# Six expert-weight slots, shared norm statistics, tanh for sigmoid, the first conv tap on ScalarE, and new turn tables in an eight-layer kernel

## The reference, cut to what matters

```python
x = x + L0_attn(layernorm(x))   # proj 128 -> 2176; causal conv of 4 taps on 1024 channels, silu; SSD scan with
                                # state 64; times silu(z); norm over 1024; proj 1024 -> 128
x = x + L0_ffn(layernorm(x))    # xr, xk: mixes of x[t] and x[t-1]; sigmoid(xr Wr) * ((relu(xk Wk))^2 Wv)
h = layernorm(x)                # h is the input and the inner residual of the next layer
x = x + L1_attn(h)              # = h + mamba(norm(h)): conv of 4 taps on 256 channels, silu, 16 states per channel
x = x + L1_ffn(layernorm(x))    # 8 experts, top 2 of 8: gelu(x w1 + b1) w2 + b2
x = x + L2_attn(layernorm(x))   # linear attention with a running sum over tokens, 16 heads of 8
x = x + L2_ffn(layernorm(x))    # silu(x w1 s1) * (x w2 s2), gelu(h1), gelu(h2), w3
x = x + L3_attn(layernorm(x))   # silu(a) * sigmoid(b) -> xin; A, B, C from xin; scan with 16 states; rms norm; proj
x = x + L3_ffn(layernorm(x))    # 8 experts, top 2: (silu(x wg + bg) * (x wu + bu)) wd + bd
```

## Time and profile before

| | |
|---|---|
| three runs | 1398.04, 1400.70, 1400.92 us (median 1400.7) |
| span of the profiled execution | 1400.6 us; no time beyond its span is recorded for it |
| busy of the span | TensorE 1104.8, VectorE 890.9, ScalarE 630.4, GpSimd 281.7 us |
| moved | 107 MB |

### The profile page before, as it was taken

One profiled execution on the slowest core, in us unless ns is written; L12 is line 12 of the kernel. 1 busy time (PEld: TensorE's weight loads), 2 busy tenths in 40 slices (PEclk: granted clock), 3 DMA queues, 4 the chain that ended last, 5 costly groups with the idle time before them and its releaser, 6 DMA issues.

```text
span 1400.6 us, 15057 instructions
## 1 busy us (share of the span) xinstructions
PE 1104.8 (79%) x4959; PEld 698.7 (50%) x4959; DVE 890.9 (64%) x1919; ACT 630.4 (45%) x1194; POOL 281.7 (20%) x258
## 2 busy tenths in 40 slices
PE   4978657767977979686768676799999899897791
PEld 2536312334743634353457442574555556787781
DVE  6787879987558767767635789723735652363432
ACT  3433385424552348634237972273252434542330
POOL 3000113324120002130230244202000032014404
PEclk9999877777989999878889897999999999899996
DMA  8100000003520000000125420370000014468782
GB/s 322 47 0 1 0 0 0 0 1 118 163 61 1 0 0 1 0 0 0 45 92 177 131 74 21 96 224 21 1 1 0 1 63 132 157 214 283 260 277 69
DMA packets 49411, 107.02 MB, mean 76 GB/s; under 512 B 4840, under 2 KB 32368, under 8 KB 48688
## 3 DMA queue, kind: packets, MB, share of 16 engines
q1 hardware_dynamic: 44656, 92.74, 20.7%
q0 software_dynamic: 4096, 8.40, 2.0%
q10 hardware_dynamic: 576, 4.87, 0.8%
HBM read 91.24 MB, written 14.75 MB: 76 GB/s over the span
## 4 chain that ended last, share of the span: by engine, by line
PE 41%; DVE 22%; ACT 13%; issue 9%; POOL 7%; DMA 6%; SPq 1%; DVEq 0%; POOLq 0%; ACTq 0%
PE ps L1920 6%; PE ps L1638 5%; DMA expert_ring<-in_e_dram 4%; PE ps L1586 4%; PE ps L1752 4%; DVE up L1341 3%; PE ps L1858 3%; POOL slots_dram L717 3%; ACT big L957 2%; PE ps L1692 2%; PE ps L1829 2%; PE ps L1958 2%; DVE big L1348 2%; POOL up L727 2%; PE ps L1909 1%
## 5 line engine op out<-in xcount | busy, mean ns | idle before, releaser
L1858 PE MATMUL ps<-big,expert_ring 128*128 128x128 f32 x1160 | 158.0, 286 | 33.6 <-DMA expert_ring<-in_e_dram 20.4
L1858 PEld LDWEIGHTS ps<-big,expert_ring 128*128 128x128 f32 x1160 | 145.2, 199 | 48.0 <-DMA expert_ring<-in_e_dram 26.9
L1341 DVE TENSOR_TENSOR_SCAN up<-cv,big 128x512 f32<-128x512 f32 x128 | 152.5, 1230 | 21.5 <-ACT cv L908 17.4
L660 POOL TENSOR_TENSOR rstd<-ve,nhalf 128x4 f32<-128x4 f32 (+1 forms) x41 | 47.2, 1153 | 577.2 <-DVE ve L1119 470.6
L1752 PE MATMUL ps<-big,consts 128*128 128x512 f32 x256 | 154.3, 735 | 2.4 <-DVE big L1348 2.4
L697 POOL TENSOR_TENSOR big<-big,mt 128x512 f32<-128x512 f32 x64 | 85.8, 1344 | 279.1 <-ACT mt L901 152.6
L1920 PE MATMUL ps<-big,weights 128*128 128x512 f32 x256 | 115.4, 597 | 0.0
L1769 PE MATMUL ps<-q,row_pick 96*128 96x512 bf16 x128 | 54.5, 448 | 76.6 <-DVE big L1348 61.4
L1829 PE MATMUL ps<-expert_ring,big 128*128 128x128 f32 x792 | 107.6, 280 | 5.9 <-ACT big L957 3.6
L1829 PEld LDWEIGHTS ps<-expert_ring,big 128*128 128x128 f32 x792 | 98.9, 195 | 15.3 <-ACT big L957 9.8
L1459 DVE SCALAR_TENSOR_TENSOR big<-ps,expert_ring,key 128x128 f32<-128x128 f32 x184 | 51.8, 344 | 79.6 <-PE ps L1858 67.4
(11 more groups left out here) (247 smaller groups left out, 1943.4 us busy)
## 6 DMA issues: line engine op xcount, KB each, us to landing
expert_ring<-in_e_dram SPq DMA_DIRECT2D x46, 836.0 KB, 5.3
expert_ring<-in_e_dram SPq DMA_DIRECT2D x53, 578.0 KB, 4.4
big<-slots_dram SPq DMA_DIRECT2D x21, 256.0 KB, 3.5
results_dram<-mt SPq DMA_DIRECT2D x21, 256.0 KB, 5.3
weights<-in_w_dram ACTq DMA_DIRECT2D x1, 3072.0 KB, 15.5
slots_dram<-big SPq DMA_DIRECT2D x2, 1024.0 KB, 10.3
weights<-in_w_dram SPq DMA_DIRECT2D x1, 1600.0 KB, 8.6
x<-in_x_dram SPq DMA_DIRECT2D x4, 256.0 KB, 13.6
```

The lines of the kernel that those rows point to most:

```text
L1341: dve.tensor_tensor_scan(UP[s][:, j, PAD:PAD + T], CV[s][:, j, :], BIG2[s][:, j, :], 0.0, ALU.mult, ALU.add).then_inc(m_scan[s], 1)
L1858: last = pe.matmul(bank4(s, r if m else b % 2)[:, k, :], ring[:, q % RING, r * T + k * P:r * T + (k + 1) * P], XGT[s][:, b // 4 % 4, b % 4 ...
```

## The change

- Layer 7 may use six weight slots, four of the ring and two in the memory of the first weights (layers 0 and part of 1). `ring_plan` gives each load the slot whose last load is oldest; layer 3 keeps to four. A load waits for the result of the block that had the slot, or, for a spare slot's first use, for the end of layer 1 for the last samples.
- In layer 7 of stream 1 the odd blocks put gate and up into stream 0's banks, once stream 0 has made its last gated product. The waits for a free bank go back two blocks there.
- In layer 2 both norms come from one set of statistics of x: the second's variance is worked out as var (1 + eps) + eps^2. GpSimd does both powers from it.
- ScalarE does the first conv tap (scale and bias) for layers 0 and 2, right behind its copy to UP. VectorE does three taps.
- sigmoid(x) becomes tanh(x / 2) in layers 1 and 6; the 0.5 and + 1 go into instructions that follow, into W_A, W_B, W_C and the norm weight (scaled once), and into the mean of squares.
- Some yields that stood ahead of a wait alone are gone, and all turn tables are new.

```diff
+def ring_plan():
+    order, held, used, plan = expert_loads(), [None] * (RING + SPARE), [0] * (RING + SPARE), {}
+    place = {load: k for k, load in enumerate(order)}
+    for load in order:
+        slots = range(RING + SPARE * load[0])
+        slot = min(slots, key=lambda k: -1 if held[k] is None else place[held[k]])
+        used[slot] += 1
+        plan[load] = slot, used[slot], held[slot]
+        held[slot] = load
+    return plan
...
+        def expert_slot(m, s, b):
+            slot = plan[m, s, b][0]
+            if slot < RING:
+                return ring[:, slot, :]
+            return W[:, (slot - RING) * EW[1]:(slot - RING + 1) * EW[1]]
...
+        def expert_bank(m, s, r, b):
+            if m and s % NS == 1 and b % 2:
+                return bank(s - 1, r)
+            return bank(s, r if m else b % 2)
...
-                            if q >= RING:
-                                pm, pi, pb = loads[q - RING]
+                            if previous:
+                                pm, pi, pb = previous
                                 sp.wait_ge(moe[pm].y[pi], moe[pm].y.at(pi, pb))
+                            elif slot >= RING:
+                                for i in range(NB - NS, NB):
+                                    sp.wait_ge(x_done[1][i], x_done[1].at(i, 0))
...
-                yield from ln(n2o, s)
-                yield from ln(n2, s)
+                for n, at in ((n2, NC), (n2o, 0)):
+                    yield
+                    pool.wait_ge(n.var[s], n.var.at(s, 0))
+                    pool.tensor_tensor(rstd[s][:, at:at + NC], ve[s][:, at:at + NC], nhalf[:, 0:NC], ALU.pow)\
+                        .then_inc(n.rs[s], 1)
...
-                        act.activation(UP[s][:, b % 2, PAD:PAD + T], bank(s, b % 2), ACT.Copy).then_inc(l0_up[s], 1)
+                        act.activation(UP[s][:, b % 2, PAD:PAD + T], bank(s, b % 2), ACT.Copy)
+                        if b >= 2:
+                            act.wait_ge(l0_xt[s], l0_xt.at(s, b - 2))
+                        act.activation(CV[s][:, b % 2, :], bank(s, b % 2), ACT.Identity, bias=pr("conv0_b", b),
+                                       scale=pr("conv0_w", 4 * b + 3)).then_inc(l0_up[s], 1)
...
-                act.activation(BIG1[s][:, 6, :], bank(s, 1), ACT.Sigmoid).then_inc(f0_sg[s], 1)
+                act.activation(BIG1[s][:, 6, :], bank(s, 1), ACT.Tanh, scale=0.5).then_inc(f0_sg[s], 1)
...
-                    act.activation(UP[s][:, j, PAD:PAD + T], bank(s, 2 + j), ACT.Sigmoid).then_inc(s_slg[s], 1)
+                    act.activation(UP[s][:, j, PAD:PAD + T], bank(s, 2 + j), ACT.Tanh, scale=0.5)\
+                        .then_inc(s_slg[s], 1)
...
-                step(dve.tensor_scalar(v[:, j, :], u[:, j, PAD:PAD + T], pr(*wcol(3)), pr(*bcol), ALU.mult, ALU.add))
...
-                yield from norm(n2o, s, (X[s], XN[s]))
-                yield
-                dve.wait_ge(n2o.done[s], n2o.done.at(s, 0))
-                yield from norm(n2, s, (XN[s], XH[s]))
+                for c in range(NC):
+                    last = dve.bn_stats(stat[s][:, c, 0, :], X[s][:, c, :])
+                step(last)
+                for c in range(NC):
+                    last = dve.bn_aggr(mv[s][:, c, :], stat[s][:, c, 0, :])
+                step(last)
+                dve.tensor_scalar(ve[s][:, NC:2 * NC], mv[s][:, 0:NC, 1], 1.0 + LN_EPS, LN_EPS * LN_EPS, ALU.mult,
+                                  ALU.add).then_inc(n2.var[s], 1)
+                dve.tensor_scalar(ve[s][:, 0:NC], mv[s][:, 0:NC, 1], LN_EPS, None, ALU.add).then_inc(n2o.var[s], 1)
+                for n, at, dst in ((n2, NC, XH[s]), (n2o, 0, XN[s])):
+                    yield
+                    dve.wait_ge(n.rs[s], n.rs.at(s, 0))
+                    for c in range(NC):
+                        last = dve.tensor_scalar(dst[:, c, :], X[s][:, c, :], mv[s][:, c, 0:1],
+                                                 rstd[s][:, at + c:at + c + 1], ALU.subtract, ALU.mult)
+                    last.then_inc(n.done[s], 1)
...
-                                pe.wait_ge(ring_in[q % RING], 16 * (q // RING + 1))
+                                pe.wait_ge(ring_in[slot], 16 * use)
                                 if b % 4 == 0:
                                     pe.wait_ge(g.gt[s], g.gt.at(s, b // 4))
-                                if m and b:
-                                    pe.wait_ge(g.act[s], g.act.at(s, b - 1))
-                            elif b:
-                                pe.wait_ge(g.h[s], g.h.at(s, b - 1))
+                            free = g.h if r else g.act
+                            if m and s % NS == 1 and b == 1:
+                                pe.wait_ge(g.h[s - 1], g.h.at(s - 1, NBLK - 1))
+                            elif m and b > s % NS:
+                                pe.wait_ge(free[s], free.at(s, b - 1 - s % NS))
```

More of the change, by code:

```diff
@@ L1450, in experts_silu @@
                 for b in range(NBLK):
[L1451 removed]
+                    bias = expert_slot(1, s, b)[:, 1540:1544]
                     yield
@@ L1845, in layer @@
                                 yield from turn_slots(g, s, k)
-                        q = loads.index((m, s, b))
+                        slot, use, _ = plan[m, s, b]
                         for r in range(m + 1):
```

96 lines of the change are left out of this document (47 added, 49 removed), and 63 rows, old and new, of the table RUNS.

## The result

The changed kernel takes 1384.8 us (median of 10 runs, 1378.33 to 1392.40); the kernel before, run beside it, 1396.96. The ratio is 0.9915 with a 95% interval of 0.9894 to 0.9936, so the gain is 0.85%, about 12 us. It lies inside the range of 1346 to 1394 that leaves out 2 in 10, but outside the band of 1350 to 1374 around the forecast of 1365, which meant three times that gain. The profiled execution took 1386.63 us, of which 1384.8 are its span. All medians here are over every execution but one: of the twelve in the last repeat of the changed kernel one took 2852.7 us, and it is left out.

The account below looks back on a forecast made before the run. No engine is full and the limit changes by stage (TensorE, VectorE, weight loads at the end). Terms -11 - 6 - 8 - 3 - 8 = -36 take 1400.6 to 1365 us; band 1350 to 1374, range leaving out 2 in 10 1346 to 1394.

Parts of the forecast that it names:

- The marks named for it: Last 90 us: no TensorE wait over 1 us on an expert load, and the 23 blocks in 70 to 76 us.
- The second term: Layer 7 of stream 0: two of 23 blocks move behind stream 1's routing, -6 us (bounds 0 and -14).
- The transfer rival: Last expert layer: transfers become the bound; at 283 GB/s 1376 us. Small gain, shared with the TensorE rival: chance 0.18.
- the first term: Last expert layer, stream 1: six slots and spare banks end most load waits, -11 us (bounds -4 and -16).
- The rest of the tables: Whole kernel: the remaining new turn order, with the same order of layers over both streams, 0 us with +-8.
- The rival with the fixed order: Whole kernel: engines stand at badly placed new handovers; 18 of 70 would give 1422 us. Slower: chance 0.10.
- Its sign: Prediction wrong if new waits over 3 us appear between the streams, above all ScalarE's in front of VectorE's conv.
- the statistics at -8: State-space layers: one statistics pass for both norms saves 2.9 us per sample, -8 us in all (bounds -3 and -13).
- tanh at -8: ScalarE: tanh for sigmoid and the new ScalarE order remove table loads, -8 us (bounds -3 and -14).
- TensorE-bound throughout: Outside 150 to 290 us matmuls cover the other engines' savings: -23 us, 1377. Small gain, shared with transfers: chance 0.18.
- The tap: Conv: first tap moved from VectorE to ScalarE, +2.5 us in 12 places, -5.7 in 10; -3 us (bounds -12.8 and +15.6).
- the band kept for a small gain: Whole kernel: 1374 to 1396 us, bound by transfers or by TensorE, chance 0.18.

Follow-up runs that it names:

- i4: The changed kernel itself, run again on the same chip as i1: 1385.6 us, ratio 0.9936 to the kernel before.
- i1: Control, repeating f2: the changed kernel with the old turn tables until about 1170 us, the new ones after: 1371.9 us, ratio 0.982.
- f1: The changed kernel with the old turn tables on all five engines until about 300 us, the new ones after: 1372.5 us, ratio 0.9826.
- f2: The changed kernel with the old turn tables on all five engines until about 1170 us, the new ones after: 1371.0 us, ratio 0.980.
- g3: The version of f2 with the sigmoids back in place of tanh: 1373.2 us, ratio 0.983 to the kernel before.
- e3: The kernel before with the first conv tap on ScalarE alone, old turn tables: ratio 0.9981 to the kernel before.

## Why the prediction was wrong

**The last stage: right, and larger than forecast.** Terms one and two were -17 together. The runs give 6.4 for slots and banks in the old order and 15.6 for the new order there, 22. The marks named for it came: no load wait over 1 us, and 71.3 us for 23 blocks (70 to 76). The second term's reason came as well, with three blocks moved where I had counted two. The transfer rival at 283 GB/s is out, with 332 GB/s from 1280 to 1310 us and the period at 2.68 us; the DMA share there is 0.98, so little is left. Wrong inside it: nothing came from the banks, as argued, but the first term took the slots as a matter of lead alone. Their use hangs on when SyncE is free to issue, which I had seen for the stores of results and not for the two stores of the output, 13.1 us of standing in the old order.

**First step that failed: "The rest of the tables. I give it 0, with +-8."** I put all of the order's good into the terms of the last stage and none of its possible harm anywhere. The part before the last stage costs 12 to 14 us (16 by the ratios of i4 and i1): stream 1's first feed-forward is 10 us late, and scans run beside GpSimd's products. That the order of the first 300 us costs this is shown by f1; which instruction in it costs what is read from traces. The argument that the order of layers is the same in both tables is true and tells nothing, since the loss comes from a few instructions of one stream put ahead of the other's. The rival with the fixed order had the mechanism, but not its size or place: 12 to 14 us, not 57, in a version that otherwise wins. Its sign came too: VectorE's longest waits for ScalarE ahead of the conv are 3.7 and 4.1 us, for 3.4 and 2.8 before. And the two state-space layers did not get 5 us shorter: from stream 0's first feed-forward to the end of its layer 2 it is 149.3 us for 149.5.

**Second step that failed: the statistics at -8 and tanh at -8.** Together they brought 2.5 us alone (interval -1.8 to 6.7) and, taken back singly, 1 to 3 and 1 to 4. The durations were right. The statistics take 2.9 us per sample off one stream's chain, and I counted most of that for all four samples; what came is about my bound of -3, sample 0 alone. That the other stream's work covers the rest is argued, not shown. For tanh I took 45% of the table loads as on the path, since 46 of 92 stand on the chain. But the chain is one path of two streams that run nearly level. In f2's version 78 loads stand behind the setup, in g3 90: 12 x 1.283 = 15.4 us of ScalarE, for which 1 to 4 us came, about a quarter at most. Taking a piece out of the longest path brings only what the next longest leaves. The rival "TensorE-bound throughout" gave statistics, tap and tanh together a third of 19, 6.3 us; alone they brought 5.1. It had their size; that TensorE is what covers them no run shows.

**The count of loads.** I gave 81, 79 or 71 by whether tanh stands alone or goes with exp or with silu. The changed kernel's trace has 69, none of them at a line with tanh. Those are its first groups:

```profile
L949 ACT ACT_TABLE_LOAD x18 | 23.1, 1283 | 0.3
L996 ACT ACT_TABLE_LOAD x15 | 19.2, 1283 | 0.3
```

The walk through the turns gives 69, and 15 at gelu, if tanh goes with silu, gelu and exp alike. ScalarE's timeline shows two of the three. The call ahead of a tanh is silu six times and gelu once, and no load stands between. Here the tanh (L1042) follows the silu (L1038), and the other (L906) stands between two gelus (L996):

```profile
585.52 0.60 ACT L1038 ACTIVATE cv<-ps 128x512 f32<-128x512 f32 x1 [0.26 <-PE ps L1980]
586.71 0.60 ACT L1042 ACTIVATE up<-ps 128x512 f32<-128x512 f32 x1 [0.59 <-PE ps L1980]
```
```profile
743.33 1.14 ACT L996 ACTIVATE big<-ps,expert_ring 128x128 f32<-128x128 f32 x4
744.33 0.63 ACT L906 ACTIVATE big<-ps 128x512 f32<-128x512 f32 x1
744.80 1.18 ACT L996 ACTIVATE big<-ps,expert_ring 128x128 f32<-128x128 f32 x4
```

The Trainium skill (ScalarE: Activation LUTs, section Table sets: the hidden batching unit) names tanh in the sets of exp and sigmoid alone; the trace shows it with silu and gelu as well, and it decides. No tanh follows an exp directly here, so for exp it shows nothing.

**The tap: right in size, as far as the noise lets one say.** Forecast -3, alone 2.6 us (interval -1.0 to 6.3), taken back from f2's version 4 to 7. In the trace of e3 the first layer ends 1.9 us later (145.7 for 143.8) and stream 1's first state-space layer 0.6 us earlier (364.7 for 365.3), so the term's loss and its gain both show. ScalarE's tap takes 0.775 us (0.779 forecast), and VectorE waits for it: 39.6 us of idle before the first tap that it still does, for 25.7 before, against 22.8 of work gone.

```profile
L1199 DVE SCALAR_TENSOR_TENSOR cv<-up,params,cv 128x512 f32<-128x512 f32 x40 | 29.9, 748 | 39.6 <-ACT cv L837 32.1 <-ACT cv L914 7.3
```

**Busy times.** I forecast 863 for VectorE and 634 to 648 for ScalarE. The control i1, with all edits, has 863.9 and 637.6. The changed kernel has 870.4 and 621.5: the scans' 6.5 us on the one, nine table loads fewer (11.5 us) on the other. So ScalarE's order was better in table loads than the old one, and between 300 and 1170 us, where seven of the nine fall away, the new order as a whole won nothing.

**The sum, redone.** 6.4 + 2.6 + 2.5 for the edits and 15.6 for the late order make 27; less 12 to 14 for the early order it is 13 to 15, measured 12. Against the forecast of 36 the two failed steps take 26 to 28 off (12 to 14, and 13.5 of the 16), and the last stage gives 5 back. That 1384.8 falls into the band kept for a small gain is luck: that band stood for a bound by transfers or by TensorE, and the loss came from neither. The version with the old order until 1170 us and the new one after it beats both kernels: 1371.0 and 1371.9 us in two sessions, ratios 0.980 and 0.982.

## What to carry to other kernels

- Where engines run in an order written down beforehand, an edit of the work and an edit of the order are two changes. Cut the order at a state that both versions pass and time the parts: here one part cost 12 to 14 us, another won 15, and together they looked like next to nothing.
- A piece's share of the longest chain bounds what its removal brings from above. Here, with two streams, table loads held 45% of their time on that chain and about a quarter of what was removed came at most.
- More buffers help only from the moment at which the issuing queue is free to fill them. Look at what that queue stands in before counting the buffers' lead.

## What the runs showed of the hardware

- A scan of 128x512 on VectorE (1.19 us) and a product of 128x512 on GpSimd (1.27 us) hold each other up where they overlap: the one that starts second ends 1.06 to 1.09 us after the first has ended (17 of 18 overlaps). Two scans behind products took 1.97 and 2.21 us, two products behind scans 2.18 and 2.05, all in the trace of the changed kernel.
- On ScalarE a tanh behind a silu or a gelu needed no load of a function table in any of seven places (changed kernel).
- The same kernels ran slower in one session than in the next on the same chip. In the pair of traces below the loss lies in one stretch. The version with the norms one after the other, first in the slow session (span 1404.8), then in the next (1371.8), over 90 us from the first scatter on:

```profile
1245.00:1335.00 90.00, 62.39 (x447) 60.45 (x446) 29.35 (x112) 23.61 (x79) 30.63 (x32) 0.79 0.66 225
```
```profile
1242.00:1332.00 90.00, 83.81 (x714) 82.31 (x714) 43.74 (x166) 36.41 (x124) 30.62 (x32) 0.96 0.95 335
```

At the end of layer 5 of sample 3, at 1171.6 and 1170.3 us, the two had been level. In the slow one VectorE and ScalarE stand for up to 15.6 and 11.7 us at a time with no wait that the profile can name. What it was stays open.
